# Attention maxima that are computed two groups early: a second copy of one head on the other half of the rows

## The chip, the cores and the metric

The kernel runs on one core of a Trainium2 chip. The metric is the device time of one execution in microseconds; the time before is the median of three runs.

## What is computed

A small network over 8 batches: a patch embedding with a short Fourier transform, an attention layer with 8 heads, a mixture of experts, a recurrent block and a second mixture of experts. The change lies in the attention layer alone. Cut to that:

```python
h = _L0_tok_ref(x, L0_tok_W)
h = jnp.concatenate([h, txt], axis=1)          # 8 batches, 1056 rows, 64 columns
h = h + _L0_attn_ref(_layernorm(h, axis=-1), ...)

def _L0_attn_ref(x, w_qkv, b_qkv, w_out, b_out):
    HEADS = 8
    b, n, d = x.shape
    scale = d ** (-0.5)
    qkv = x @ w_qkv + b_qkv
    q, k, v = (to_heads(t) for t in jnp.split(qkv, 3, axis=-1))
    dots = jnp.einsum('bhid,bhjd->bhij', q, k) * scale
    attn = jax.nn.softmax(dots, axis=-1)
    out = jnp.einsum('bhij,bhjd->bhid', attn, v)
    return out.transpose(0, 2, 1, 3).reshape(b, n, d) @ w_out + b_out
```

## The kernel before

The attention stage is `attend_stage`. The 64 heads (8 batches, 8 heads of 8 columns) are worked on in 16 **groups** of four heads. Group j belongs to batch j // 2 and lies on the partitions (rows) 0 to 63 if j is even and 64 to 127 if j is odd. Queries and keys of a group stand in `b_q` and `b_k`, two buffers each, one per batch in turn. Each value is split into three bf16 parts, whose six products are stacked on 48 rows of the contraction; three more rows hold the negated row maximum for the scores, again in three parts. So a maximum's matmul contracts over 48 rows and a score's over 51, both of one half of the 128 rows.

A group has two kinds of work on TensorE.

- **Scores.** A group has 69 **units** (`UNITS`). Units 0 to 31 and 33 to 64 are one 128 x 512 block of exponents each: two matmuls (L986) with 64 columns of weights and 512 of data. Units 32 and 65 are the text keys (L990), units 66 to 68 the text queries (66 and 67: sixteen matmuls of 128 columns of weights and 32 of data, L995; 68: four small ones, L999). Each unit goes into one of three buffers of `b_p_s`, ScalarE takes the exp of it (L823), and after a block of units `weigh` multiplies the probabilities by v (L1014, L1021) into `b_p_o`.
- **Maxima.** The row maximum of every row must be known before a group's scores can run, since the score's matmul subtracts it. A group has 32 maximum **slots** x = 0 to 31, each 128 rows of one head (x // 8 is the head) against 1024 keys: `piece` (L941) with k = 0 and 1, two matmuls each, fills the two banks of one of two buffers of `b_p_m`, and VectorE reduces them to one column (L846). Three further slots treat the text keys (L961) and text rows (L966). When all are done, VectorE makes the negated maximum in three bf16 parts (L857 to L865), TensorE transposes them (slot `TURN`, L970), VectorE copies them out (L872) and `send_max` on SP's queue brings them by DRAM to the three rows of `b_q`.

The order is written out by hand. While group j's units run, the slots of group j+1 are spread among them: `paired_at(U, ...)` puts the bank k = 0 of a slot ahead of the score of unit U and the bank k = 1 ahead of that of unit U+1, and `by_itself_at(U, ...)` puts a whole slot behind unit U's score. The first slots of a group are done one group earlier still. With `HEAD = 7` they are x = 0 to 6, all of them rows of the group's first head, and the last slots of group j+1 end with unit 50. So in group j come, in this order: x = 31 of group j+1 at units 49 and 50; for an even j from 2 the slot `JOIN` behind unit 52 (the output projection of the previous batch, L630, added on VectorE); x = 0 and 1 of group j+2 at units 53 to 56; `TURN` of group j+1 behind unit 56; x = 2 at units 57 and 58; x = 3 and 4 at units 61 to 64; x = 5 behind unit 66; x = 6 behind unit 67. Groups j and j+2 lie on the same half of the rows, groups j and j+1 on different ones.

A slot waits (`rows_ready`) until the reduction of the slot two before it has freed its buffer (`rows_free`), a score (`score_ready`) until the exp of three units before has. VectorE's reduction of a paired slot waits for the score of its second unit (`scored`).

On SP's queue, each step j of the loop sends the maximum of group j+1 (`send_max`), for an odd j starts the join of a batch (`load_sums`), waits until all units of group j are weighed (`pv_done`), loads group j+4 (`load_quad`, nine DMAs) and for an odd j sends the inverse of the sums around (`spread_inverse`, behind VectorE's reciprocal of L614).

Of the kernel before, what the change touches and what calls it, by code (L numbers as in the profile page):

```python
# [15 lines left out]
BF16 = mybir.dt.bfloat16  # L16
# [4 lines left out]
P = 128  # L21
# [5 lines left out]
SEQ = TOK + TXT  # L27
# [4 lines left out]
HEADS, DH = 8, 8  # L32
QUAD = 4
HG = HEADS // QUAD
PARTS = 3
PAIRS = [(0, 0), (0, 1), (0, 2), (1, 0), (1, 1), (2, 0)]
SHARE = [(0, 3), (3, 2), (5, 1)]
KS = len(PAIRS) * DH
# [521 lines left out]
def attend_stage(g, v_all, own, steps, late_ctx):  # L560

    nc = g.nc
    NQ = B * HG
    QN = SEQ - TOK
    WIDE = 512
# [8 lines left out]
    END = [max(u for u in range(US) if UNITS[u][0] == a) + 1 for a in range(SUMS)]  # L574
    MS = FULL_ROWS + 3
    half_in = [[g.sem(f"b_half_in{s}{q}") for q in range(HG)] for s in range(2)]
    sums_clear = g.sem("b_sums_clear")
    ones_set = [g.sem(f"b_ones_set{s}") for s in range(2)]
    max_sent, max_in = g.sem("b_max_sent"), [g.sem(f"b_max_in{q}") for q in range(HG)]
    rows_full, rows_free, max_step, max_copied = g.sem("b_rows_full"), g.sem("b_rows_free"), g.sem("b_max_step"), g.sem("b_max_copied")  # L580
# [10 lines left out]
    def load_sums(sp, b):  # L591

        e = b % 2
        for k in range(2):
            sp.wait_ge(sum_sent[k], 16 * SUMS * (b + 1))
        rows = g.sum_scr[b, :, :, :].rearrange("p (i r) t -> r (p i) t", r=32)
        sp.dma_start(den[:, :], rows[DH, :, :].rearrange("h (s n) -> h s n", n=SPAN)).then_inc(den_in, 16)
        if b >= 2:
            sp.wait_ge(att_ready, b - 1)
        sp.dma_start(num[e * D:e * D + D, :], rows[0:DH, :, :].rearrange("d h t -> h d t")).then_inc(num_in, 16)  # L600

    def spread_inverse(sp, b):

        e = b % 2
        sp.wait_ge(inverted, b + 1)
        sp.dma_start(g.inv_scr[b, :, :].rearrange("h (s n) -> (h s) n", n=SPAN), inv[:, :]).then_inc(inv_sent, 16)
        sp.wait_ge(inv_sent, 16 * (b + 1))
        sp.dma_start(inv_wide[e * D:e * D + D, :], g.inv_scr[b, :, :].unsqueeze(1).to_broadcast([HEADS, DH, SEQ])).then_inc(inv_in, 16)
# [32 lines left out]
    with ExitStack() as c:  # L641
        sb = lambda n, s, d=F32: c.enter_context(nc.sbuf_tensor(n, s, d))
        ps = lambda n, s: c.enter_context(nc.psum_tensor(n, s, F32))
        q_st = [sb(f"b_q{s}", [P, QUAD, SEQ], BF16) for s in range(2)]
        k_st = [sb(f"b_k{s}", [P, QUAD, SEQ], BF16) for s in range(2)]
        prob = sb("b_prob", [P, PR_RING, WIDE])
        m3 = sb("b_m3", [P, ROWS, 2])
        neg_max = sb("b_neg_max", [P, ROWS])
# [14 lines left out]
        HEAD = 7  # L663
# [50 lines left out]
        slot_of = {step: X for X, step in enumerate(SLOTS)}  # L714
# [3 lines left out]
        def load_quad(sp, b, p):  # L718
            s = b % 2
            heads = slice(p * QUAD, p * QUAD + QUAD)  # L720
            for k, (qa, _) in enumerate(PAIRS):
                r = 64 * p + k * DH
                sp.dma_start(q_st[s][r:r + DH, :, :], g.qk_scr[b, 0, heads, qa, :, :].rearrange("h d t -> d h t")).then_inc(half_in[s][p], 16)
            r = 64 * p
            for lo, n in SHARE:
                sp.dma_start(k_st[s][r + lo * DH:r + (lo + n) * DH, :, :],
                             g.qk_scr[b, 1, heads, 0:n, :, :].rearrange("h a d t -> (a d) h t")).then_inc(half_in[s][p], 16)

        HALF_IN = 16 * (len(PAIRS) + len(SHARE))

        def send_max(sp, j):
            b, p = divmod(j, HG)
            s, r = b % 2, 64 * p + KS
            sp.wait_ge(max_copied, j + 1)
            sp.dma_start(g.max_scr[j, :, :, :].rearrange("a r i -> r a i"), max_row[:, :, :]).then_inc(max_sent, 16)
            sp.wait_ge(max_sent, 16 * (j + 1))
            for a in range(PARTS):
                sp.dma_start(q_st[s][r + a:r + a + 1, :, 0:TOK],
                             g.max_scr[j, a:a + 1, 0:FULL_ROWS, :].rearrange("a (h t) i -> a h (t i)", t=FULL)).then_inc(max_in[p], 16)
            sp.dma_start(q_st[s][r:r + PARTS, :, TOK:SEQ],  # L740
                         g.max_scr[j, :, FULL_ROWS, :].rearrange("a (q i) -> a q i", q=QUAD)).then_inc(max_in[p], 16)
# [3 lines left out]
        @block.sync  # L745
        def _(sp):
            for b in range(2):
                sp.wait_ge(ones_set[b], 2)
                for p in range(HG):
                    load_quad(sp, b, p)  # L750
            for e in range(2):
                sp.dma_start(w_out[e * D:e * D + D, :], g.arg["L0_attn_w_out"]).then_inc(w_in, 16)
            sp.dma_start(bias[:, :], g.arg["L0_attn_b_out"].rearrange("(a d) -> a d", a=1).to_broadcast([P, D])).then_inc(w_in, 16)
            load_experts, load_biases, spread_out, spread_in, _ = sync_steps(sp)
            send_max(sp, 0)
            for j in range(NQ):
                b, p = divmod(j, HG)
                if j + 1 < NQ:
                    send_max(sp, j + 1)
                joins = p == HG - 1 and b + 1 < B  # L760
                if joins:
                    load_sums(sp, b)
                if b + 2 < B:
                    sp.wait_ge(pv_done, US * (j + 1))
                    load_quad(sp, b + 2, p)
                if joins:
                    spread_inverse(sp, b)
                if j == NQ - 3:
                    load_experts()
                if j == NQ - 1:  # L770
                    load_biases()
                    spread_out(0)
                    spread_in(0, (0,))
# [149 lines left out]
        def _(pe):  # L923
            def rows_ready(j, x):
                X = slot_of[j, x]
                if x == 0:
                    pe.wait_ge(half_in[j // HG % 2][j % HG], HALF_IN * (j // HG // 2 + 1))
                if x == TURN:
                    pe.wait_ge(max_step, 6 * j + 6)
                if X >= 2:  # L930
                    pe.wait_ge(rows_free, X - 1)

            def piece(j, x, k):

                b, p = divmod(j, HG)
                s = b % 2
                r = slice(64 * p, 64 * p + KS)
                out = p_m[:, slot_of[j, x] % 2, :, :]
                i, t = divmod(x, FULL)
                for e in range(0, P, 64):  # L940
                    last = nc.tensor.matmul(out[e:e + 64, k, :], q_st[s][r, i, t * P + e:t * P + e + 64], k_st[s][r, i, k * WIDE:k * WIDE + WIDE],  # L941
                                            start=True, stop=True)
                return last

# [85 lines left out]
            for j in range(NQ):  # L1030
                b, p = divmod(j, HG)
                pe.wait_ge(max_in[p], MAX_IN * (b + 1))
                lo = 0
                for u in range(US):
# [19 lines left out]
                    if u in LAST:  # L1054
                        block.append((j, lo, u + 1))
                        lo = u + 1
# [1289 lines left out]
```

## Time and profile before

| | us |
|---|---|
| median of 3 runs | 1983.98 |
| lowest and highest | 1983.07 and 1994.29 |
| the profiled execution | 1982.23 |
| its span | 1980.4 |
| TensorE matmul busy | 1776.4 (90%) |
| VectorE busy | 1264.6 (64%) |
| ScalarE busy | 1046.2 (53%) |

A group is counted from the exp of its unit 0 to that of the next group's. Busy time is the sum of the time in which an engine has an instruction under way, over the span. Matmuls are pipelined, so a busy TensorE can have room. The attention's groups run from about 212 to 1027 us of the span. In a group of instructions, the last columns are the idle time of the engine just before them and what ended most of it: that is the time in which the engine was short of input. Times in the timelines are from the span's start.

### The profile page before, as it was taken

How to read it: one execution, taken by the hardware profiler on the slowest of the kernel's cores; microseconds unless marked ns; L12 is line 12 of the kernel's file. 1: busy time of each engine (PE TensorE's matmuls, PEld its weight loads, DVE VectorE, ACT ScalarE, POOL GpSimd, SP SyncE). 2: the span in 40 equal slices, each digit the busy share in tenths (PEclk: the TensorE clock that was granted, in tenths of full speed). 3: DMA queues.
4: the chain of work that ended last, by engine and by line, in shares of the span. 5: the costliest groups of instructions: out<-in, count | busy, mean ns of one | idle time of the engine just before them, and what ended most of it. 6: DMA issues, size and time to landing. Idle time of an engine off the chain costs nothing. (4 is left out here: it accounts for less than half of the span.)

```text
span 1980.4 us, 41031 instructions
## 1 busy us (share of the span) xinstructions
PE 1776.4 (90%) x15515; PEld 761.0 (38%) x15515; DVE 1264.6 (64%) x3179; ACT 1046.2 (53%) x1967; POOL 347.4 (18%) x332
## 2 busy tenths in 40 slices
PE   5856899999999999999989999997389996999998
PEld 2321222222222222222224444443179974444443
DVE  1457988888788787878716778864556653434331
ACT  1330577777677676767665555553133332555554
POOL 1222000000000000000101356546102443000000
PEclk9975899999899999989999999997789996999999
DMA  5624011111111111100127675530120002242241
GB/s 193 222 70 67 7 30 42 30 42 30 37 30 42 30 37 35 33 23 19 33 66 149 122 137 100 104 75 3 38 60 21 1 1 45 52 93 52 51 83 30
DMA packets 86754, 115.83 MB, mean 58 GB/s; under 512 B 29934, under 2 KB 70984, under 8 KB 84512
## 3 DMA queue, kind: packets, MB, share of 16 engines
q1 hardware_dynamic: 81964, 104.03, 24.6%
q0 software_dynamic: 3104, 8.72, 1.2%
q8 instruction: 126, 2.06, 0.4%
q14 instruction: 68, 0.56, 0.1%
q10 hardware_dynamic: 1492, 0.46, 0.1%
HBM read 94.35 MB, written 18.82 MB: 57 GB/s over the span
## 5 line engine op out<-in xcount | busy, mean ns | idle before, releaser
L823 ACT ACTIVATE b_prob<-b_p_s 128x512 f32<-128x512 f32 x1104 | 570.6, 604 | 306.0 <-PE b_p_s L986 289.5
L846 DVE TENSOR_REDUCE b_m<-b_p_m 128x1 f32<-128x1024 f32 x512 | 604.2, 1219 | 143.0 <-PE b_p_s L986 109.9
L941 PE MATMUL b_p_m<-b_k,b_q 48*64 48x512 bf16 x2048 | 374.7, 416 | 53.2 <-DMA b_k<-qk_scr 22.8
L986 PE MATMUL b_p_s<-b_q,b_k 51*64 51x512 bf16 x2048 | 356.8, 397 | 8.5 <-ACT b_prob L823 7.9
L1014 PE MATMUL b_p_o<-b_prob,v_all 128*9 128x512 f32 x2304 | 309.1, 620 | 0.9
L941 PEld LDWEIGHTS b_p_m<-b_k,b_q 48*64 48x64 bf16 x2048 | 94.4, 108 | 432.2 <-DVE b_m L846 254.5
L1388 ACT ACTIVATE d_hidden<-d_p_z 128x704 f32<-128x704 f32 x192 | 135.1, 754 | 102.4 <-PE d_p_z L1298 102.3
L1388 ACT ACTIVATE n_hidden<-n_p_z 128x704 f32<-128x704 f32 x192 | 135.0, 754 | 99.4 <-PE n_p_z L1298 99.2
L801 POOL DMA_DIRECT2D sum_scr<-b_sums x48 | 26.3, 548 | 768.7 <-ACT b_sums L813 768.5
L1526 DVE TENSOR_TENSOR d_xg<-d_xd,d_c_wide 128x352 f32<-128x352 f32 x192 | 113.1, 626 | 66.4 <-PE d_p_z L1298 32.4
L1298 PE MATMUL d_p_z<-d_xg,d_w 64*128 64x352 f32 x768 | 142.4, 486 | 0.0
L1298 PE MATMUL n_p_z<-n_xg,n_w 64*128 64x352 f32 x768 | 142.2, 485 | 0.0
L1311 PE MATMUL n_p_y<-n_hidden,n_w 128*64 128x352 f32 x768 | 134.6, 472 | 0.0
L1311 PE MATMUL d_p_y<-d_hidden,d_w 128*64 128x352 f32 x768 | 134.6, 472 | 0.0
L986 PEld LDWEIGHTS b_p_s<-b_q,b_k 51*64 51x64 bf16 x2048 | 95.3, 105 | 58.1 <-ACT b_prob L823 43.5
L1298 PEld LDWEIGHTS d_p_z<-d_xg,d_w 64*128 64x128 f32 x768 | 69.3, 187 | 48.5 <-ACT d_hidden L1388 22.6
L1298 PEld LDWEIGHTS n_p_z<-n_xg,n_w 64*128 64x128 f32 x768 | 69.2, 187 | 48.3 <-ACT n_hidden L1388 22.0
L1526 DVE TENSOR_TENSOR n_xg<-d_xn_all,m_x_all 128x352 f32<-128x352 f32 x96 | 47.4, 518 | 47.7 <-DMA m_x_all<-n_c_scr 21.6
L1311 PEld LDWEIGHTS n_p_y<-n_hidden,n_w 128*64 128x64 f32 x768 | 46.7, 136 | 76.2 <-issue 62.5
L1311 PEld LDWEIGHTS d_p_y<-d_hidden,d_w 128*64 128x64 f32 x768 | 46.7, 136 | 76.2 <-issue 62.5
L1014 PEld LDWEIGHTS b_p_o<-b_prob,v_all 128*9 128x9 f32 x2304 | 38.2, 90 | 74.9 <-issue 59.4
L265 PE MATMUL a_p_a<-xt,w_fold 64*64 64x512 f32 x512 | 62.3, 610 | 1.1 <-DVE w_fold L442 1.1
(354 smaller groups left out, 2106.1 us busy)
## 6 DMA issues: line engine op xcount, KB each, us to landing
d_c_wide<-d_c_scr SPq DMA_DIRECT2D x48, 704.0 KB, 13.3
m_x_all<-n_c_scr SPq DMA_DIRECT2D x48, 352.0 KB, 8.4
xt<-in_x SPq DMA_DIRECT2D x16, 1024.0 KB, 8.8
sum_scr<-b_sums POOLq DMA_DIRECT2D x32, 256.0 KB, 2.3
b_q<-qk_scr SPq DMA_DIRECT2D x96, 66.0 KB
qk_scr<-a_qk_part SPq DMA_DIRECT2D x24, 256.0 KB, 2.8
k_rate<-rate_scr SPq DMA_DIRECT2D x8, 528.0 KB, 4.5
b_k<-qk_scr SPq DMA_DIRECT2D x16, 198.0 KB
```

The lines of the kernel that those rows point to most:

```text
L265: last = nc.tensor.matmul(p_tok[half * D:half * D + D, e, :], w_fold[r, k, :, :].rearrange("p j i -> p (j i)"), col, start=(k == 0), stop= ...
L801: pool.dma_start(g.sum_scr[b, p, :, a * WIDE:a * WIDE + w], sums[:, n % 2, 0:w]).then_inc(sum_sent[n % 2], 16)
L823: nc.scalar.activation(prob[:, U % PR_RING, 0:w], p_s[:, U % S_RING, 0:w], ACT.Exp, scale=float(D) ** -0.5).then_inc(exp_done, 1)
L846: nc.vector.tensor_reduce(m3[:, x, 0:1], p_m[:, s, :, :].rearrange("p k n -> p (k n)"), axis=AX.X, op=ALU.max).then_inc(rows_free, 1)
L941: last = nc.tensor.matmul(out[e:e + 64, k, :], q_st[s][r, i, t * P + e:t * P + e + 64], k_st[s][r, i, k * WIDE:k * WIDE + WIDE], start=Tru ...
L986: last = nc.tensor.matmul(out[e:e + 64, :], k_st[s][r, q, jt * P + e:jt * P + e + 64], q_st[s][r, q, a * WIDE:a * WIDE + WIDE], start=True ...
L1014: last = nc.tensor.matmul(p_o[32 * i:32 * i + DH + 1, :], v[:, jt, p * QUAD + i, :], prob[:, slot, :], start=(jt == 0), stop=(jt == FULL), ...
L1298: last = nc.tensor.matmul(own["p_z"][:, n % 2, q, 0:CH], w1[r, pr, f * P:f * P + P], own["xg"][r, n // HALVES % XR, :], start=True, stop=True)
L1311: last = nc.tensor.matmul(own["p_y"][q * D:q * D + D, 0:CH], w2[:, 2 * pr + q, f, :], own["hidden"][:, n % HR, q, :], start=(k == 0), stop ...
L1388: nc.scalar.activation(own["hidden"][:, n % HR, :, :], own["p_z"][:, n % 2, :, 0:CH], ACT.Relu).then_inc(relu_done, 1)
L1526: nc.vector.tensor_tensor(own["xg"][:, j % XR, :], own["xd"][b % 3][:, a * CH:a * CH + CH], own["c_wide"][b % 2][a][:, pr, :], ALU.mult)\
```

## The change

The seven early slots read a copy. Two new tiles, `b_q_head` and `b_k_head` of [128, 1056] bf16, hold the first head of a group on the half of the rows opposite to the group's own. `load_head(sp, j)` fills the half for group j in six DMAs on SP's queue: three for the queries (each part is repeated on as many row blocks as it has products) and three for the keys. It is called once for group 2 before the loop and then in step j for group j+3, behind `load_quad` and before `spread_inverse`; from group 4 on it waits until the last reader of the same half, slot 6 of group j-2, is done. `from_copy` is true for x < 7 of groups 2 to 15, and there `piece` takes its operands from the copy. TensorE waits for the copy (`head_in`) at x = 0 and for the group's own load (`half_in`) at x = 7. The groups 0 and 1 keep their way. The count, order and shapes of all matmuls stay.

```diff
     half_in = [[g.sem(f"b_half_in{s}{q}") for q in range(HG)] for s in range(2)]
+    head_in = [g.sem(f"b_head_in{q}") for q in range(HG)]
...
+        q_head, k_head = sb("b_q_head", [P, SEQ], BF16), sb("b_k_head", [P, SEQ], BF16)
...
+        HEAD_IN = 16 * 2 * len(SHARE)
+
+        def from_copy(j, x):
+            return j >= HG and x < HEAD
+
+        def load_head(sp, j):
+            b, p = divmod(j, HG)
+            h, r = p * QUAD, 64 * (1 - p)
+            if j >= 2 * HG:
+                sp.wait_ge(rows_free, slot_of[j - HG, HEAD - 1] + 1)
+            for a, (lo, n) in enumerate(SHARE):
+                sp.dma_start(q_head[r + lo * DH:r + (lo + PARTS - a) * DH, :],
+                             g.qk_scr[b, 0, h, a, :, :].unsqueeze(0).to_broadcast([PARTS - a, DH, SEQ])).then_inc(head_in[p], 16)
+                sp.dma_start(k_head[r + lo * DH:r + (lo + n) * DH, :],
+                             g.qk_scr[b, 1, h, 0:n, :, :].rearrange("a d t -> (a d) t")).then_inc(head_in[p], 16)
...
             load_experts, load_biases, spread_out, spread_in, _ = sync_steps(sp)
+            load_head(sp, HG)
             send_max(sp, 0)
...
                     load_quad(sp, b + 2, p)
+                if j + HG + 1 < NQ:
+                    load_head(sp, j + HG + 1)
                 if joins:
                     spread_inverse(sp, b)
...
-                if x == 0:
+                if x == 0 and from_copy(j, x):
+                    pe.wait_ge(head_in[j % HG], HEAD_IN * (j // HG))
+                if x == (HEAD if j >= HG else 0):
                     pe.wait_ge(half_in[j // HG % 2][j % HG], HALF_IN * (j // HG // 2 + 1))
...
+                q, keys = q_st[s][r, i, :], k_st[s][r, i, :]
+                if from_copy(j, x):
+                    r = slice(64 * (1 - p), 64 * (1 - p) + KS)
+                    q, keys = q_head[r, :], k_head[r, :]
                 for e in range(0, P, 64):
-                    last = nc.tensor.matmul(out[e:e + 64, k, :], q_st[s][r, i, t * P + e:t * P + e + 64], k_st[s][r, i, k * WIDE:k * WIDE + WIDE],
+                    last = nc.tensor.matmul(out[e:e + 64, k, :], q[:, t * P + e:t * P + e + 64], keys[:, k * WIDE:k * WIDE + WIDE],
                                             start=True, stop=True)
```

## Rows read from the trace of the kernel before

**Rows 1.** The page, busy time and share of the span of each engine.

```profile
PE 1776.4 (90%) x15515; PEld 761.0 (38%) x15515; DVE 1264.6 (64%) x3179; ACT 1046.2 (53%) x1967; POOL 347.4 (18%) x332
```

**Rows 2.** The page, costliest groups: busy us, mean ns | idle before, releasers.

```profile
L823 ACT ACTIVATE b_prob<-b_p_s 128x512 f32<-128x512 f32 x1104 | 570.6, 604 | 306.0 <-PE b_p_s L986 289.5
L846 DVE TENSOR_REDUCE b_m<-b_p_m 128x1 f32<-128x1024 f32 x512 | 604.2, 1219 | 143.0 <-PE b_p_s L986 109.9
```

**Rows 3.** Stretches (groups 2, 5, 6, 7; two falls): us, busy by engine, clock, DMA.

```profile
311.32:362.99 51.67, 47.78 (x587) 14.73 (x581) 42.55 (x44) 36.38 (x73) 4.06 (x4) 1.00 0.18 41
465.13:514.40 49.27, 45.60 (x570) 12.75 (x563) 41.41 (x41) 36.39 (x73) 1.66 (x3) 1.00 0.15 30
514.40:569.05 54.65, 51.84 (x586) 15.10 (x581) 42.63 (x44) 36.38 (x72) 4.04 (x4) 0.91 0.18 39
569.05:619.93 50.88, 47.21 (x570) 12.85 (x563) 41.41 (x41) 36.40 (x73) 1.66 (x3) 0.97 0.14 29
...
954.40:957.70 3.30, 3.30 (x20) 0.43 (x16) 1.03 (x2) 0.00 (x0) 0.00 (x0) 0.50 0.93 125
432.10:435.40 3.30, 3.30 (x24) 0.50 (x16) 1.78 (x2) 1.06 (x3) 0.00 (x0) 0.50 0.26 82
```

**Rows 4.** Timeline of TensorE in the steady part: start us, length, engine, line.

```profile
521.24 0.40 PE L941 MATMUL b_p_m<-b_k,b_q 48*64 48x512 bf16 x2
521.25 0.40 PE L986 MATMUL b_p_s<-b_q,b_k 51*64 51x512 bf16 x2
```

**Rows 5.** Timeline of TensorE in group 5 from unit 53 on.

```profile
500.40 0.40 PE L941 MATMUL b_p_m<-b_k,b_q 48*64 48x512 bf16 x2
500.64 0.38 PE L986 MATMUL b_p_s<-b_q,b_k 51*64 51x512 bf16 x2
500.86 0.38 PE L941 MATMUL b_p_m<-b_k,b_q 48*64 48x512 bf16 x2
...
502.87 0.33 PE L970 MATMUL b_p_m<-eye_bf,b_max_part 128*33 128x128 bf16 x3 [0.54 <-DVE b_m L846]
...
504.10 0.40 PE L941 MATMUL b_p_m<-b_k,b_q 48*64 48x512 bf16 x2
...
510.38 0.62 PE L941 MATMUL b_p_m<-b_k,b_q 48*64 48x512 bf16 x4
510.93 0.56 PE L995 MATMUL b_p_s<-b_q,b_k 51*128 51x32 bf16 x16
```

**Rows 6.** Timeline of ScalarE in group 5 from unit 53 on.

```profile
501.06 2.07 ACT L823 ACTIVATE b_prob<-b_p_s 128x512 f32<-128x512 f32 x4 [0.56 <-PE b_p_s L986]
...
507.39 2.56 ACT L823 ACTIVATE b_prob<-b_p_s 128x512 f32<-128x512 f32 x5 [0.56 <-PE b_p_s L986]
```

**Rows 7.** Timeline of VectorE in group 5 around unit 53.

```profile
500.91 0.20 DVE L865 TENSOR_TENSOR b_max_part<-b_max_rest,b_max_part 128x33 bf16<-128x33 f32 x1
501.50 2.36 DVE L846 TENSOR_REDUCE b_m<-b_p_m 128x1 f32<-128x1024 f32 x2 [0.39 <-PE b_p_s L986]
```

**Rows 8.** Group 14, without early slots: ScalarE's timeline, and the stretch to its end.

```profile
970.29 2.06 ACT L823 ACTIVATE b_prob<-b_p_s 128x512 f32<-128x512 f32 x4 [2.49 <-PE b_p_s L986]
...
975.37 2.56 ACT L823 ACTIVATE b_prob<-b_p_s 128x512 f32<-128x512 f32 x5 [0.34 <-PE b_p_s L986]
...
970.29:981.12 10.83, 9.97 (x109) 2.98 (x107) 7.07 (x41) 7.87 (x17) 2.57 (x3) 1.00 0.02 5
```

**Rows 9.** Timeline of VectorE in group 2, slot 0 of group 4.

```profile
350.09 2.36 DVE L846 TENSOR_REDUCE b_m<-b_p_m 128x1 f32<-128x1024 f32 x2 [1.16 <-PE b_p_s L986]
```

**Rows 10.** Timeline of SP's queue in group 6, and the DMA issues by kind.

```profile
523.57 1.25 SPq L726 DMA_DIRECT2D b_k<-qk_scr  x3
532.06 0.34 SPq L606 DMA_DIRECT2D inv_scr<-c_inv  x1
...
b_q<-qk_scr SPq DMA_DIRECT2D x96, 66.0 KB
b_k<-qk_scr SPq DMA_DIRECT2D x16, 198.0 KB
```

## The prediction

> **What bounds the kernel now.** I read the page's busy shares first, then the groups of instructions, the busy time in stretches, and last the timelines of one group of heads. TensorE is busy 90% of the span [rows 1], but its matmuls are pipelined, so that alone says little. The groups say more: in the attention stage ScalarE's exp was idle 306.0 us before its instructions, 289.5 of it until a score of L986 was done, and VectorE's row maximum of L846 was idle 143.0 us, 109.9 of it for the same line [rows 2]. So there are places where both wait for TensorE. The stage is 16 groups j (two per batch), each of 69 units. A group without disturbance takes 49.27 us when j is odd and 51.67 us when j is even, where the even one also joins the output of an earlier batch [rows 3].
>
> Most of a group is not TensorE's. In the steady part a maximum slot for group j+1 reads the other half of the rows than the scores of group j, and the two run side by side: the maximum's matmuls start at 521.24 and the score's at 521.25 [rows 4]. Two slots then cost VectorE 2 x 1.22 us for four units, more than the 2.07 us that ScalarE takes for the four exps [rows 2, 6]. That is VectorE's pace and it stays.
>
> The change touches the last 17 units of groups 0 to 13. Units 53, 55, 57, 61 and 63 start a pair of units with one of the slots x = 0 to 4 of group j+2, and units 66 and 67 are each followed by one (x = 5 and 6). Group j+2 lies on the same row half as group j. The timeline of j = 5 shows the price: maximum at 500.40, score at 500.64, maximum at 500.86 [rows 5], in turn and some 0.22 to 0.24 us each, where the steady part has them at one time.
>
> **The change part by part.** Unit 53 comes first. Its score no longer stands behind a bank of the maximum, so it starts at 500.40 and not at 500.64, and its exp at 500.82 and not 501.06: 0.24 us sooner [rows 5, 6].
>
> Slot 0's maximum is taken when both its banks and unit 54's score are there, at 501.50, which is 0.42 us behind the start of that score. With the banks beside the scores, that score starts at about 500.64, and the maximum could start at 501.06. In an odd group VectorE is until 501.11 at the five small steps that make group j+1's negated maximum [rows 7], so it starts near 501.15: 0.35 us sooner. In an even group VectorE has waited for 1.16 us when slot 0 comes [rows 9], so all of 0.44 us is gained.
>
> What follows hangs on that maximum: the transposes (slot TURN) start at 502.87, 0.14 us after it has ended and freed its buffer, then the weighing with v (L1014), then unit 57 at 504.10 [rows 5, 7]. All of it moves by 0.35 or 0.44 us. Behind the second maximum there is little room left: it would end at about 503.5, and unit 57 would start at 503.7.
>
> Units 57 to 60 have one slot. Unit 57's score starts with the unit and not 0.24 us into it. Unit 60's score waits for unit 57's exp, the weighing stands behind it, and unit 61 starts behind that, so unit 61 too starts 0.24 us sooner than its share of the shift before. In unit 61 the same 0.24 us comes once more, for the score that leads its exp. From exp 61 on, units 61 to 65 go at ScalarE's pace: five exps in 2.56 us, without idle time [rows 6]. The slots 3 and 4 cost nothing there now and give nothing back when they are hidden.
>
> Sum for a group: 0.35 + 0.24 + 0.24 = 0.83 us for an odd one and 0.44 + 0.48 = 0.92 us for an even one. Seven of each give 5.8 + 6.4 = 12.2 us. Group 14 is a check, because group 16 does not exist and it has no such slots: its exp 61 follows exp 53 by 975.37 - 970.29 = 5.08 us [rows 8]; in group 5 it is 507.39 - 501.06 = 6.33 us [rows 6], and my sum makes that 5.7 us, between the two, as it should be with VectorE's share still there.
>
> Units 66 to 68 are the open part. There a slot's four matmuls (64 columns of weights) stand between sixteen score matmuls of another form (128 columns of weights, 32 columns of data). They start at 510.38 and the next sixteen at 510.93 [rows 5]. Two banks and the stream of the last take 0.24 + 0.21 = 0.45 us, so 0.10 us more is lost here than between a score and a maximum of one form on one half, which follow each other at 0.22 us. No row shows two forms on two halves at one time. The bounds are nothing, if a change of form lets nothing overlap, and about 0.35 us for each of two slots (0.55 less what issuing takes), which is 9.8 us over 14 groups. The extra 0.10 us is a sign that a change of form waits for the array, so I take nothing. The Trainium skill, "TensorEngine Tiling (Array Packing)", section Tiling Modes, says of tiles that "Mode switching requires drain"; by it the sum stays at 12.2 us, and without it it would be 22.0. That 0.10 us agrees with it but does not prove it for two halves.
>
> The outer bound on all of it is group 14's tail: from exp 53 to the next group's first exp it takes 10.83 us, against 514.40 - 501.06 = 13.34 us [rows 3, 6, 8]. That is 2.5 us, and 35 us over 14 groups, but it leaves out VectorE's seven maxima as well, which the change keeps. At the other end lies nothing gained.
>
> The loads are added to SP's queue: six DMAs a group, 198 KB together (two times 48 rows of 2112 bytes), a quarter of the 792 KB that load_quad moves (six loads of b_q of 66 KB, and as much in three of b_k). They go behind load_quad, whose last issue ends at 524.82, and ahead of spread_inverse, whose first issue is at 532.06, right after VectorE's reciprocal [rows 10]. Six at some 0.4 us end by 527.3, so nothing is late; if they did run on, the inverse would move, and it is first used in the join of units 49 to 52. send_max of the next group waits for VectorE until near the group's end. Each head is loaded some 13 us into the group whose unit 53 reads it, where slot 0's maximum starts 350.09 - 311.32 = 38.8 us into it [rows 3, 9]; that leaves some 25 us for the transfer. The buffer's half was last read two groups earlier, so the new waits of SP and TensorE are open when they are reached. If that cover were gone, unit 53 would be late and all engines with it. The head that is loaded before the first group is issued while the maxima of group 0 run. No gain and no loss from any of this. POOL's queue is untouched; the half_in wait of TensorE moves seven slots later, when that load is long in.
>
> One thing works against the sum: TensorE's clock. From 432.10 to 435.40 and in seven more places of the stage, the last from 954.40 to 957.70, it was 0.50 of full, the lower level, 1.2 GHz. Group 7 was at 0.97 on the mean and took 50.88 us and not 49.27; group 6 was at 0.91 and took 54.65 us and not 51.67 [rows 3]. So a fall costs 1.6 to 3.0 us. Before these falls the engine did the text units and slots with their many 32-column matmuls, and waited for VectorE. The places of the falls depend on where the groups come to lie in time. Shorter groups move the places. I see no reason for more or fewer on the mean, and take zero, with three falls either way (about 5 us) as the spread.
>
> The profiled execution took 1982.23 us, 1980.4 of it the span; 12.2 less is 1970.0. It lies 1.75 us below the median of 1983.98, so the median's counterpart is 1971.8 us.
>
> **The rivals.** First, the tail overlaps too: another 9.8 us, 22.0 in all, 1962.0 us. For it speaks that two halves are free of each other at 3 ns in the steady part; against it the 0.10 us above. Second, VectorE is next at once: its chain of small steps and two maxima holds unit 57 where it is, and only the two times 0.24 us are left: 6.7 us, 1977.3 us. For it speaks that VectorE's gap before slot 0 is only 0.39 us in odd groups; against it the 1.16 us in even ones. Third, the copy does not do what it says, and the slots still run in turn: 1984 us. The steady part speaks against it, since only the row half differs there. Fourth, the slower side, the clock: with the maxima hidden, TensorE has less to do in units 53 to 60, where it already waits for VectorE before the transposes. If its clock falls there in most groups, each fall costs 1.6 us; eight more falls eat up the gain, and one in each of the 14 groups gives 22.4 - 12.2 = 10.2 us more, 1994 us. For it speaks that the waits there resemble those ahead of the falls in the text part; against it that group 14, with fewer matmuls still, was at full clock from 970.29 to 981.12 [rows 8]. The Trainium skill, "TensorE: Matmul & The Clock Gate", section HAM oscillation, warns that idle gaps between bursts of matmuls lower the clock; that rule speaks against this change, and by it the time would be the 1994 us of this rival.
>
> **How the numbers follow.** The forecast has 0.55, the overlapping tail 0.17, VectorE next 0.12, no overlap 0.05, the clock 0.11. The time is that of the first, 1971.8 us; its own range is 1966 to 1978. The range of all goes from 1960 (the tail overlaps, and a fall less) to 1985 (nothing is gained, or some falls more), and leaves out about 0.15, the larger part of it on the clock's side. About 1% is what a measurement of this kernel tells from no change, which is 1964.1 and 2003.8 us. Faster by more needs most of the tail or several falls fewer: 0.17. Slower by more needs a fall in each group and something on top: 0.02. Within it: 0.81.
>
> **What would show it.** In units 53 to 64 of groups 0 to 13 the maximum and the score start within some nanoseconds of each other. Undisturbed odd groups take 48.4 us and even ones 50.8 us. The transposes start about 2.5 us after unit 53 does. Behind unit 66 the next sixteen score matmuls still start 0.55 us after the slot's four; at about 0.2 us the first rival is right. If unit 57 stays 3.70 us behind unit 53, it is VectorE. If the clock in units 53 to 60 is at half in many groups, it is the fourth. The prediction is wrong as a whole if the groups keep their length.

## The result, and the profile after

The changed kernel took 1971.27 us in the median of 5 runs (1962.17 to 1992.39). The kernel before took 1988.69 us in the 5 runs by then (1983.07 to 1994.29). The ratio is 0.989, with a 95% interval of 0.9865 to 0.9916. Beside it on another chip, the medians were 1974.41 us (10 runs) and 1992.40 us (29 runs), a ratio of 0.991 (0.988 to 0.994).

Two executions of the changed kernel were profiled: first the longest of these five runs, which a mean granted clock of 0.926 slowed to 1992.39 us, and second one of 1970.26 us at 0.940 (the profile before has 0.942). A **fall** is a stretch in which TensorE's granted clock is at its lower level.

From the page of the second profile, the two groups of instructions that answer to [rows 2]:

```profile
L843 ACT ACTIVATE b_prob<-b_p_s 128x512 f32<-128x512 f32 x1104 | 570.5, 602 | 290.4 <-PE b_p_s L1012 273.7
L866 DVE TENSOR_REDUCE b_m<-b_p_m 128x1 f32<-128x1024 f32 x512 | 604.2, 1219 | 121.5 <-PE b_p_s L1012 86.6
```

VectorE's maxima lost 143.0 - 121.5 = 21.5 us of waiting, part of it because this execution had fewer falls. Next, stretches of the first profile (us, busy time by engine, granted clock, DMA): groups 2, 3, 4 and 6, and the longest of the falls in groups 0 to 13. They answer to [rows 3].

```profile
312.80:369.76 56.96, 53.14 (x588) 14.84 (x581) 42.52 (x44) 36.37 (x73) 4.06 (x4) 0.85 0.19 40
369.76:418.14 48.38, 43.88 (x568) 11.86 (x563) 41.37 (x41) 36.38 (x72) 1.66 (x3) 1.00 0.18 35
418.14:471.57 53.43, 49.18 (x587) 14.14 (x581) 42.52 (x44) 36.38 (x72) 4.05 (x4) 0.94 0.21 43
...
519.96:570.75 50.79, 46.07 (x587) 13.85 (x581) 42.53 (x44) 36.37 (x72) 4.04 (x4) 1.00 0.22 46
350.60:364.00 13.40, 12.89 (x81) 2.95 (x80) 5.68 (x8) 5.53 (x11) 0.00 (x0) 0.50 0.03 5
```

At full clock a group takes 48.38 us where it took 49.27, and 50.79 where it took 51.67: 0.88 us less for either kind, 12.3 us over 14 groups. Group 2 is the other side. It had two falls, a short one 24 us into the group and a long one from 37.8 us on (350.60 to 364.00), right behind the join's matmuls. Together they made the group 6.2 us longer than group 6.

The second profile had two such groups, 12 and 14. For comparison, the last line is group 14 of the kernel before:

```profile
808.29:862.32 54.03, 50.18 (x587) 14.31 (x581) 42.53 (x44) 36.37 (x72) 4.06 (x4) 0.91 0.20 46
910.71:966.91 56.20, 53.18 (x553) 14.25 (x547) 42.51 (x78) 36.16 (x72) 9.16 (x8) 0.82 0.18 34
```

```profile
930.53:981.12 50.59, 46.41 (x553) 13.52 (x547) 41.07 (x77) 36.17 (x73) 6.62 (x7) 0.97 0.19 38
```

Group 12 lost 3.2 us by its two falls. Group 14 has no early slots, so the change edits nothing in it, and still it takes 5.6 us more than before: a fall of 17 us behind its join, in both profiles. So the 12.0 us between the two spans (1980.4 and 1968.4) are not the shorter groups alone. Groups 0 to 13 together went from 718.9 to 697.7 us, 21.2 us less: 12.3 by their length, some 9 because only two of them had falls where seven had. Groups 14 and 15 gave 5.7 us of that back, and the stages around the attention 3.5.

The second profile shows the same end of group 5 as [rows 5 to 7]. ScalarE, from unit 49 on:

```profile
495.69 2.07 ACT L843 ACTIVATE b_prob<-b_p_s 128x512 f32<-128x512 f32 x4 [0.36 <-PE b_p_s L1012]
498.11 2.07 ACT L843 ACTIVATE b_prob<-b_p_s 128x512 f32<-128x512 f32 x4 [0.35 <-PE b_p_s L1012]
501.39 2.07 ACT L843 ACTIVATE b_prob<-b_p_s 128x512 f32<-128x512 f32 x4 [1.22 <-PE b_p_s L1012]
503.81 2.56 ACT L843 ACTIVATE b_prob<-b_p_s 128x512 f32<-128x512 f32 x5 [0.35 <-PE b_p_s L1012]
506.85 0.60 ACT L843 ACTIVATE b_prob<-b_p_s 128x512 f32<-128x512 f32 x1 [0.48 <-PE b_p_s L1021]
```

VectorE, the small steps' last and the slots 0 and 1:

```profile
498.16 0.20 DVE L885 TENSOR_TENSOR b_max_part<-b_max_rest,b_max_part 128x33 bf16<-128x33 f32 x1
498.32 2.35 DVE L866 TENSOR_REDUCE b_m<-b_p_m 128x1 f32<-128x1024 f32 x2
```

TensorE, in group 5 (units 53 to 57) and in group 6 (units 66 and 67):

```profile
497.64 0.40 PE L967 MATMUL b_p_m<-b_k_head,b_q_head 48*64 48x512 bf16 x2
497.65 0.40 PE L1012 MATMUL b_p_s<-b_q,b_k 51*64 51x512 bf16 x2
...
499.69 0.33 PE L996 MATMUL b_p_m<-eye_bf,b_max_part 128*33 128x128 bf16 x3 [0.53 <-DVE b_m L866]
...
500.93 0.40 PE L967 MATMUL b_p_m<-b_k_head,b_q_head 48*64 48x512 bf16 x2
...
557.04 0.56 PE L1021 MATMUL b_p_s<-b_q,b_k 51*128 51x32 bf16 x16
557.54 0.62 PE L967 MATMUL b_p_m<-b_k_head,b_q_head 48*64 48x512 bf16 x4
558.09 0.56 PE L1021 MATMUL b_p_s<-b_q,b_k 51*128 51x32 bf16 x16
```

Maximum and score of unit 53 now start 0.01 us apart. VectorE takes slot 0 with no idle time, straight from the last of its small steps. Behind unit 66 nothing has moved: the four matmuls of the slot start, and the next sixteen start 0.55 us later, as before.

SP's queue in group 6:

```profile
519.72 1.07 SPq L728 DMA_DIRECT2D b_k<-qk_scr  x3
520.83 0.76 SPq L743 DMA_DIRECT2D b_q_head<-qk_scr  x1
...
523.73 0.29 SPq L745 DMA_DIRECT2D b_k_head<-qk_scr  x1
528.42 0.35 SPq L607 DMA_DIRECT2D inv_scr<-c_inv  x1
```

The six issues take 3.2 us (520.83 to 524.02) and end 4.4 us ahead of the inverse.

### The profile page after: what moved, and what is told of

It reads as the page before. It is cut to its first block and busy times, and to the rows that moved or that the text cites. A ratio compares the mean times of both kernels' runs of the same rounds, so it can differ in the third digit from the quotient of the medians.

```text
span 1990.6 us, 41131 instructions
## 1 busy us (share of the span) xinstructions
PE 1778.2 (89%) x15515; PEld 763.2 (38%) x15515; DVE 1264.3 (64%) x3179; ACT 1046.0 (53%) x1967; POOL 346.2 (17%) x332
## 5 line engine op out<-in xcount | busy, mean ns | idle before, releaser
L967 PE MATMUL b_p_m<-b_k,b_q 48*64 48x512 bf16 x1656 | 302.4, 422 | 52.8 <-DMA b_k<-qk_scr 22.2
L1040 PE MATMUL b_p_o<-b_prob,v_all 128*9 128x512 f32 x2304 | 313.6, 628 | 0.8
L967 PEld LDWEIGHTS b_p_m<-b_k,b_q 48*64 48x64 bf16 x1656 | 75.3, 109 | 377.0 <-DVE b_m L866 233.4
L967 PE MATMUL b_p_m<-b_k_head,b_q_head 48*64 48x512 bf16 x392 | 65.7, 420 | 6.2 <-ACT b_prob L843 6.2
```

The lines of the kernel that those rows point to most:

```text
L967: last = nc.tensor.matmul(out[e:e + 64, k, :], q[:, t * P + e:t * P + e + 64], keys[:, k * WIDE:k * WIDE + WIDE], start=True, stop=True)
L1040: last = nc.tensor.matmul(p_o[32 * i:32 * i + DH + 1, :], v[:, jt, p * QUAD + i, :], prob[:, slot, :], start=(jt == 0), stop=(jt == FULL), ...
```

## The experiments

All ratios are against the kernel before, measured on the same chip in turn, with their 95% interval. "Group" is the length of an undisturbed odd group, 49.27 us before and 48.39 us with the change.

**The changed kernel again.**

> The changed kernel once more, for an execution whose clock falls elsewhere and for more times. Theory (score leads the unit): undisturbed groups take 48.39 us (odd) and about 50.8 us (even) again, whatever the clock does; the span differs from the last one only by falls of TensorE's clock, whose places depend on how the groups lie in time. A time of 1962 to 1975 us with a mean clock of 0.94 or more, near 1990 with 0.93. Rival (the change itself makes the clock fall near the join): falls in units 49 to 56 of most even groups again.

Measured: 1974.41 us, ratio 0.9909 (0.9877 to 0.9941). Ten of the fourteen changed groups, 2 to 11, ran at full clock one after the other, at 48.39 and 50.79 us; falls came in groups 1 and 12, and then in 14. So the change does not by itself bring a fall at every join, and the theory holds for the lengths. That holds for groups 0 to 13; group 14 had its long fall in both profiles. The 29 runs of before on this chip show how much the clock weighs: time against mean clock is nearly a line (correlation -0.97), 15 us for 0.01. Their mean is 1992.5 us at 0.936, that of the changed kernel 1974.9 us at 0.939. Of the 17.6 us between the means, 0.0024 x 1500 = 3.7 us go with the clock and 13.9 us remain, near the 12.3 us of the groups.

**Only the loads.** The copy is loaded and waited for, but not read. Here, and in every variant below that reads the group's own half, `half_in` is waited for at x = 0 again.

```diff
-                if from_copy(j, x):
+                if False:
                     r = slice(64 * (1 - p), 64 * (1 - p) + KS)
```

> The head is loaded onto the other half and waited for, but all slots read their own half as before. Theory: the loads are hidden, the groups are back at 49.27 and 51.67 us, ratio to before 1.000. Rival (the added transfers or their place in SP's queue cost time that the overlap hides): ratio above 1.003.

Measured: 1989.69 us, ratio 0.9991 (0.9961 to 1.0020). Group 3 of this kernel:

```profile
367.11:416.39 49.28, 45.61 (x570) 12.75 (x563) 41.41 (x41) 36.37 (x73) 1.66 (x3) 1.00 0.16 35
```

The group keeps its length (49.28 us), so neither the loads nor the added wait cost anything that can be measured.

**Which slots give the gain.** In one kernel the five paired slots read the copy, in the other the two slots of the tail.

```diff
-                if from_copy(j, x):
+                if from_copy(j, x) and x < 5:
```

> Only the five paired slots x = 0 to 4 read the copy; the two slots behind units 66 and 67 read their own half. Theory (a change of the matmul's form lets nothing overlap): the groups keep 48.39 and about 50.8 us, all of the gain is here, ratio about 0.993. Rival (part of the gain is in the tail): groups 0.1 us or more longer than with all seven.

```diff
-                if from_copy(j, x):
+                if from_copy(j, x) and x >= 5:
```

> Only the two slots behind units 66 and 67 read the copy. Theory: nothing gained, groups 49.27 and 51.67 us, ratio 1.000. Rival: groups shorter by 0.1 us or more.

Measured: 1971.71 us, ratio 0.9911 (0.9878 to 0.9945), for the five; 1990.97 us, ratio 1.0005 (0.9973 to 1.0037), for the two. Group 5 of the first and group 5 of the second:

```profile
462.31:510.70 48.39, 43.88 (x570) 11.84 (x563) 41.38 (x41) 36.38 (x73) 1.67 (x3) 1.00 0.18 35
```

```profile
483.96:533.24 49.28, 45.61 (x571) 12.75 (x563) 41.41 (x41) 36.38 (x73) 1.66 (x3) 1.00 0.18 34
355.21:382.32 27.11, 27.11 (x161) 7.12 (x160) 9.89 (x12) 9.49 (x18) 0.00 (x0) 0.50 0.01 2
```

All of the gain is in the five paired slots. The last line, from the same profile as the second group (an execution of 2010.82 us), is a stretch at half clock that began behind the join of group 2. It lasted 27 us and made that group 64.3 us long. Slots 0 to 4 are as in the kernel before there, and so is the group length, so a fall at the join does not need the hidden maxima or the shorter groups.

**The form of the tail's matmuls.** The sixteen score matmuls of units 66 and 67 become thirty-two with 64 columns of weights, the form that the slots have; the results are the same.

```diff
                         for i in range(QUAD):
-                            last = nc.tensor.matmul(out[:, ...], k_st[s][r, i, (jt + t) * P:(jt + t) * P + P], ...)
+                            for e in range(0, P, 64):
+                                last = nc.tensor.matmul(out[e:e + 64, ...], k_st[s][r, i, (jt + t) * P + e:(jt + t) * P + e + 64], ...)
```

> The changed kernel with the sixteen score matmuls of units 66 and 67 split into thirty-two of 64 columns of weights, the form that the slots have; same results. Theory (the change of form keeps the slot of the tail from overlapping): behind the last of the thirty-two the slot's first matmul starts within 0.03 us, and the next score matmul starts within some 0.05 us of the slot's last and not 0.31 us behind it. Rival (something else, as the shape of short matmuls or the buffers, keeps them apart): the gaps stay near 0.10 and 0.31 us.

Measured: 1969.64 us in 4 runs, ratio 0.9894 (0.9837 to 0.9951). TensorE in units 66 to 68 of group 5:

```profile
504.60 0.58 PE L1022 MATMUL b_p_s<-b_q,b_k 51*64 51x32 bf16 x26
505.01 0.40 PE L967 MATMUL b_p_m<-b_k_head,b_q_head 48*64 48x512 bf16 x2
505.03 0.37 PE L1022 MATMUL b_p_s<-b_q,b_k 51*64 51x32 bf16 x14
505.25 0.38 PE L967 MATMUL b_p_m<-b_k_head,b_q_head 48*64 48x512 bf16 x2
505.25 0.61 PE L1022 MATMUL b_p_s<-b_q,b_k 51*64 51x32 bf16 x24
505.70 0.62 PE L967 MATMUL b_p_m<-b_k_head,b_q_head 48*64 48x512 bf16 x4
506.25 0.20 PE L1027 MATMUL b_p_s<-b_q,b_k 51*32 51x32 bf16 x4
```

The slot's matmuls now lie inside the run of score matmuls: by the counts, 8 of unit 67's 32 have started (26 + 14 - 32) before the slot's second bank does at 505.25. The next score behind a slot of another form still waits: unit 68 keeps its 0.55 us (505.70 to 506.25), as its four matmuls have 32 columns of weights. Units 66 to 67 went from 1.04 to 0.64 us (exp to exp), units 65 to 66 from 1.12 to 1.24, and the group from 48.39 to 47.95 us. So the form kept the tail apart, and not the shortness of the matmuls or the buffers. How much of the 0.44 us is the overlap of the two halves and how much the gaps of the changing form was not taken apart: no run has one form and the slots on their own half.

**Later slots only.** Slots 0 and 1 read their own half.

```diff
-                if from_copy(j, x):
+                if from_copy(j, x) and x >= 2:
```

> Slots 0 and 1 (units 53 to 56) read their own half, slots 2 to 6 the copy. Theory (each leading score is worth 0.2 us, the earlier first maximum 0.2 to 0.4 us): the steps 49 to 53 and 53 to 57 of the exps are 2.62 and about 3.48 us, the step 57 to 61 is 2.42; a group is 48.8 us (odd), 0.4 us longer than with all seven. Rival (VectorE alone sets units 53 to 57): 48.6 us or less, since hiding slots 0 and 1 would give little.

Measured: 2006.27 us, ratio 1.0055 (1.0025 to 1.0084), slower than before. And yet its groups did what was expected: exp to exp 2.62 us for units 49 to 53, 3.51 for 53 to 57 and 2.42 for 57 to 61 in group 5, and 48.81 us for the group.

```profile
512.68 2.06 ACT L843 ACTIVATE b_prob<-b_p_s 128x512 f32<-128x512 f32 x4 [0.56 <-PE b_p_s L1012]
516.19 2.06 ACT L843 ACTIVATE b_prob<-b_p_s 128x512 f32<-128x512 f32 x4 [1.44 <-PE b_p_s L1012]
```

What made it slow is the clock. Its groups 2 and 3, and the two falls of group 2:

```profile
313.99:375.04 61.05, 57.99 (x585) 15.54 (x581) 42.73 (x44) 36.70 (x72) 4.06 (x4) 0.78 0.17 38
375.04:423.85 48.81, 44.80 (x570) 12.17 (x563) 41.31 (x41) 36.38 (x73) 1.66 (x3) 0.99 0.17 35
338.61:341.82 3.21, 3.21 (x24) 0.54 (x16) 0.28 (x2) 0.35 (x1) 0.00 (x0) 0.50 0.06 17
352.26:375.95 23.69, 23.69 (x159) 5.35 (x151) 9.90 (x11) 9.31 (x18) 0.00 (x0) 0.50 0.01 3
```

Each of the even groups 2 to 14 had a fall some 24 us in, and six of the seven another at the join, 38 us in. Three of those lasted over 23 us. (Counts like these are from one profiled execution of each kernel.) The mean clock of its runs was 0.924. So either what slots 0 and 1 do brings the falls, or the length of the groups does. The next two runs are for that.

**A longer tail.** The changed kernel, with the sixteen score matmuls of unit 67 done twice in groups 0 to 13. It has the group length of the kernel just shown, but its own slots 0 and 1.

```diff
-                    for t in range(4):
+                    for t in (range(4) if jt == 0 or j >= NQ - 2 else (0, 1, 2, 3, 0, 1, 2, 3)):
```

> The changed kernel with the sixteen score matmuls of unit 67 done twice in groups 0 to 13 (the same values again): nothing but 0.4 us more of TensorE in the tail, far from the text part and the join. The groups come to 48.8 us (odd) and 51.2 us (even), the lengths of the run where slots 0 and 1 read their own half. Theory (the cost of the clock hangs on how the group's length puts the text part and the join in time): falls in units 33 to 56 of most even groups again, a time of 1990 to 2005 us, 20 us or more over the changed kernel. Rival (that run's falls came from what slots 0 and 1 do in units 53 to 56): only the 5.6 us of the longer tails, 1979 us.

Measured: 1989.74 us, ratio 0.9994 (0.9964 to 1.0024). A group is 48.79 us. Group 4 had two falls, the second at the join:

```profile
415.59:469.80 54.21, 49.62 (x602) 14.60 (x597) 42.63 (x44) 36.38 (x72) 4.05 (x4) 0.94 0.20 43
439.96:443.17 3.21, 3.21 (x24) 0.59 (x20) 0.52 (x2) 0.00 (x0) 0.00 (x0) 0.50 0.17 68
453.61:456.82 3.21, 3.21 (x23) 0.67 (x22) 0.81 (x2) 0.28 (x1) 0.00 (x0) 0.50 0.00 0
```

A tail of 5.6 us in all costs 15 us against the changed kernel's 1974.41 (17 us by the two ratios), less than the 20 of the theory and more than the 5.6 of the rival. Six of the seven even groups from 2 to 14 have falls with nothing changed but the tail, four of them at the join. But the falls of over 20 us are missing. At one and the same group length (48.79 and 48.81 us) the mean clock was 0.932 here and 0.924 there, and groups 0 to 13 took 714 us here and 742 us there, so the length is not all of it.

**Later slots only, and the longer tail.** Both edits at once.

> Slots 0 and 1 read their own half (the kernel that was slower than before), and besides the sixteen score matmuls of unit 67 are done twice, 0.4 us more for each of 14 groups: 49.2 and 51.6 us, a pair of groups 100.8 us, close to the 100.9 of the kernel before. Theory (the lengths put the text part and the join where the clock falls): more work and less time, some 1990 to 1998 us where the kernel without the longer tail had 2005. Rival (what slots 0 and 1 do in units 53 to 56 brings the falls and keeps the clock low): 2005 + 5.6 = 2011 us, with stretches of over 20 us at the lower level again.

Measured: 1981.26 us, ratio 0.9961 (0.9935 to 0.9987). Groups 2 and 3, and the one fall of group 2:

```profile
314.60:367.89 53.29, 48.81 (x602) 14.71 (x597) 42.62 (x44) 36.38 (x72) 4.06 (x4) 0.97 0.21 43
367.89:417.11 49.22, 44.97 (x587) 12.58 (x579) 41.49 (x41) 36.38 (x73) 1.66 (x3) 1.00 0.18 34
338.57:341.79 3.22, 3.22 (x16) 0.32 (x10) 0.93 (x2) 0.00 (x0) 0.00 (x0) 0.50 0.21 73
```

With 5.6 us more to do, the kernel is 25 us faster by the medians and 19 us by the two ratios (they were taken on different chips), and faster than was expected (1990 to 1998 us). Every even group from 2 on has a fall 24 us in, and none at the join. With slots 0 and 1 done in the same way, 0.4 us more of length took the falls away from the join. So what slots 0 and 1 do does not by itself bring them. Whether it makes those that come longer, as the comparison with the longer tail alone suggests, stays open.

**More to do in the text part.** The changed kernel with the score matmuls of units 32 and 36 done twice, where TensorE waits for VectorE.

```diff
-                    for e in range(0, P, 64):
+                    for e in ((0, 64, 0, 64) if u == 36 else (0, 64)):
...
-                    for i in range(QUAD):
+                    for i in (range(QUAD) if a else [0, 1, 2, 3, 0, 1, 2, 3]):
```

> The changed kernel with the four score matmuls of unit 32 and the two of unit 36 done twice (the same values), where TensorE waits for VectorE anyway. Theory (the clock falls in the text part because TensorE has too little to do there): groups without a fall keep 48.4 and 50.8 us, falls at 20 to 25 us into a group become rare, those at the join remain; 1965 to 1975 us. Rival (falls do not depend on it): as many falls there as with the change alone, and groups up to 0.4 us longer.

Measured: 1976.14 us, ratio 0.9916 (0.9887 to 0.9946). Odd groups grew to 48.57 us, and the falls in the text part stayed: groups 1, 4, 8, 12 and 14 had one 24 us in, of the fifteen from 0 to 14. With the unpadded kernel they were 1, 12 and 14 in one profile and 0, 2, 4, 10, 12 and 14 in the other. The expected rarity of falls did not come. With 3 and 6 of them in two profiles of one kernel, the 5 here show no effect of the extra matmuls either way.

**Seven slots in other places.** With the scores no longer behind the maxima, units 57 to 60 have room for a second slot; then one slot is left behind unit 66.

```diff
-                for at in range(0, 2 if n in (12, 14) else 4, 2):
+                for at in range(0, 2 if n == 12 else 4, 2):
...
-            for u in TAIL[:-1]:
+            for u in TAIL[:1]:
```

> All seven slots read the copy; block 57 to 60 takes two slots (x = 2 and 3) and only one slot is left behind unit 66, none behind unit 67. Theory: TensorE has room in units 57 to 60 now, VectorE needs 2.44 us for two maxima where the block takes 2.42, and a slot of the tail costs TensorE 0.55 us: groups of 47.9 and 50.3 us, 7 us less in all than with the change alone, ratio near 0.987. Rival (VectorE becomes the bound of the whole end of the group): groups stay above 48.2 us.

Measured: 1970.91 us, ratio 0.9903 (0.9869 to 0.9937), group 47.84 us. The group is 0.55 us shorter, as expected, and the time is not, against 1974.41 (ratio 0.9909): the mean clock was 0.935 here and 0.939 there, and 0.003 to 0.004 of clock go with some 5 us.

With all seven slots paired (the 4 of every block, and none in the tail):

> All seven slots paired (x = 0 at units 51 and 52), none in the tail. Theory: the tail gives another 0.5 us, but in units 49 to 56 VectorE has one maximum more beside the five small steps and is the bound there, some 0.7 us longer; the groups are no shorter than with six paired, about 48.0 us. Rival (TensorE is still the bound): 47.4 us for an odd group.

Measured: 1989.18 us, ratio 0.9982 (0.9957 to 1.0007). A group at full clock takes 48.26 us, so pairing the last slot costs 0.4 us against six paired: VectorE is the bound there. Here are its maxima of the slots 0 to 2 in group 5, in one piece behind the small steps, and the copy of the transposed maximum:

```profile
508.20 0.20 DVE L885 TENSOR_TENSOR b_max_part<-b_max_rest,b_max_part 128x33 bf16<-128x33 f32 x1
508.31 3.48 DVE L866 TENSOR_REDUCE b_m<-b_p_m 128x1 f32<-128x1024 f32 x3
511.71 0.34 DVE L892 COPY b_max_row<-b_p_m 33x384 bf16<-33x384 bf16 x1
```

The odd groups are still no longer than the 48.39 us of the change, so the 15 us lost against it are the clock's, 0.926 on the mean of its runs. Five of its falls (groups 0, 1, 5, 9 and 13) begin behind unit 56, after TensorE has waited up to 1.26 us for VectorE; exp 53 to exp 57 takes 4.34 us in an undisturbed odd group there, and 3.28 with six paired. It is the place that the prediction's fourth rival named.

Six paired and the tail in one form:

> The changed kernel with six paired slots, one behind unit 66, and the tail's score matmuls in the form of 64 columns. Theory: the two shortenings add as far as one slot is left to hide: 47.84 us less about 0.2, 47.6 us for an odd group and 50.0 for an even one, 1962 to 1970 us depending on the clock. Rival (VectorE takes over): 47.84 us as with six paired alone.

Measured: 1958.95 us (1957.89 to 1962.19), ratio 0.9829 (0.9799 to 0.9860). Groups 3 and 6:

```profile
363.73:411.23 47.50, 43.18 (x602) 11.81 (x595) 41.38 (x41) 36.28 (x73) 1.66 (x3) 1.00 0.19 36
511.60:561.50 49.90, 45.36 (x618) 13.80 (x613) 42.54 (x44) 36.27 (x72) 4.05 (x4) 1.00 0.21 46
```

This is the best of all. The ratio stands for 34 us, and 24.8 us of them are group length (1.77 us in each of 14 groups). The mean clock was 0.941, and 0.933 in the runs of before beside it; by the 15 us for 0.01, that is enough for the other 9 us.

## Why the prediction was right, and where it was not

- **The sum.** 12.2 us were forecast in the groups, 12.3 came (14 x 0.88). The places were right, the sizes less so. In the odd group the step from exp 49 to exp 53 fell from 2.62 to 2.42 us. From exp 49 to exp 57 it was 6.32 us and is 5.70; to exp 61 it was 8.95 and is 8.12, 0.83 us less, as in the working. But the shift that slot 0's maximum gives is 0.42 us and not 0.35, and each of the two leading scores gives 0.20 us and not 0.24, so two errors cancel. In the even group the same three steps give 0.82 us where 0.92 was forecast. In both kinds the last 0.06 us come between units 65 and 66 (1.18 to 1.12 us), which had no term. That the totals agree to 0.1 us is in part luck.
- **VectorE as the next bound.** The forecast had VectorE's small steps hold slot 0's maximum back in the odd group. They end right at it and hold nothing back: it starts 2.63 us after exp 49, where it was 3.06, so 0.43 us sooner, and it overlaps the end of the last small step by 0.04 us instead of following it. In the even group it comes 0.42 us sooner, where 0.44 was forecast, and VectorE still waits 0.74 us for it.
- **The tail.** No gain was taken there, and none came. The reason given, a change of form that waits for the array, was an inference from 0.10 us in one half; the run with one form shows it for two halves. The rule cited from the Trainium skill ("TensorEngine Tiling (Array Packing)", Tiling Modes) agrees with this: with the mode kept, matmuls of two halves run through each other, with the mode changed the next ones start 0.55 us behind the slot's first.
- **The loads.** Six issues took 3.2 us, where 2.4 were forecast, and they were in time all the same.
- **The clock: this step was mis-sized.** I took zero on the mean and a price of 1.6 to 3.0 us for a fall, with three more or fewer as the spread. Zero on the mean nearly held: the mean clock was 0.0024 higher with the change, some 4 us in its favour. The number of falls in the stage (5 and 11 in two profiles) was at the two ends of the range (8 before). The price did not hold. It was too high at its lower end already before the change: group 4 took 52.87 us with its fall, 1.2 us more than 51.67. With the change some falls lie at the join, where none of before's eight did, and they last up to 17 us. The two falls of group 14 make it 5.6 us longer than before's group 14 with its one. The spread of 5 us was too small for single runs, which scatter by 30 us (1962 to 1992); those of the kernel before do so too (1980 to 2014).
- **The fourth rival** named units 53 to 60 and TensorE's waits there. The falls at the join begin between the exps of units 52 and 53, right behind the join's matmuls, and last into those units. But with the change they do not follow a wait of any length: in the 7 us before each of them TensorE's longest idle gap was 0.27 us, and in the whole stage of the second profile, from group 1 on, 0.53 us. So the rule on idle gaps, on which this rival also leaned, does not tell these falls; only with all seven slots paired did some falls come behind a longer wait (1.26 us), in units 56 to 60. The argument against the rival failed as well: it was that group 14 was at full clock in its end, and with the change it is at half clock there in both profiles. The runs with the longer tail show that the group length moves these falls, and the run with only the two slots of the tail shows that they can come without the hidden maxima.
- **The signs to look for.** Group lengths of 48.4 and 50.8 us are there to 0.1 us, and unit 57 is 3.29 us behind unit 53 (497.64 to 500.93), not 3.70. One sign was worked out wrongly: the transposes were to come 2.5 us after unit 53, which is the value of before (502.87 - 500.40); by the forecast's own terms it had to be 2.1, and it is 2.05.

The time forecast, 1971.8 us, was put against a median of 1983.98 us, and more runs put before at 1989 to 1996 us. The time of the change is right to 1 us partly because the runs of before that were known lay at their low end. The difference of the two profiles' spans, 12.0 us against the 12.2 forecast, is chance too: it is the sum of a shorter stage and of falls that went both ways.

What stays open: what starts a fall; why a fall at the join lasts 3 us in one kernel and 24 or 27 in another; and at which group length the falls are fewest. No kernel was tried that changes the join's matmuls.

## What to carry to other kernels

Work that TensorE does in turn only because its operands share a half of the rows can be hidden for the price of a second copy, if the two matmuls also have the same number of weight columns. Count the gain as the time by which the next engine's input comes sooner, at each place where it waits, and not as the matmul time that disappears: five slots with 0.44 us of matmuls each gave 0.88 us. On a kernel with many short waits on TensorE, compare the granted clock of both kernels' runs before a difference under 1% is read as the edit's.

## What the runs showed of the hardware

- **Two forms of matmul do not mix.** 64 columns of weights on one half and 128 on the other stand in turn, with 0.10 us and 0.31 us (0.55 - 0.24) between the starts of neighbours; with 64 on both, neighbours start within some 0.02 us (505.01 and 505.03).
- **The length of a loop step moves the clock, and in no simple way.** Nearly the same work with 0.4 us more in each group had a mean clock of 0.943 where it had 0.924, and a time of 1981 where it had 2006 us. The length does not say it alone: the rows of 48.79 and 48.81 us differ.

(The runs were made on three chips, on which before had a mean clock of 0.933 to 0.938; the ratio is to before on the same chip.)

| kernel | odd group us | median us | ratio | mean clock |
|---|---|---|---|---|
| six paired, tail in one form | 47.50 | 1958.95 | 0.983 | 0.941 |
| six paired | 47.84 | 1970.91 | 0.990 | 0.935 |
| the change | 48.39 | 1974.41 | 0.991 | 0.939 |
| the change, longer tail | 48.79 | 1989.74 | 0.999 | 0.932 |
| later slots only | 48.81 | 2006.27 | 1.006 | 0.924 |
| later slots only, longer tail | 49.20 | 1981.26 | 0.996 | 0.943 |
| before (29 runs) | 49.27 | 1992.40 | 1 | 0.936 |

- **A stretch at the lower level can be long**: some 3.3 us in most places, but up to 27 us behind the join, where TensorE was busy all through (27.11 of 27.11 us).
- **The clock fell without a long idle gap of TensorE.** In the second profile of the change it fell five times in the stage, and the longest gap from group 1 on was 0.53 us.
